# Attention and graph kernel: row sums over one accumulator, softmax weights in five groups

## What is computed

```python
# layer 0: x is (2, 2048, 512), 16 heads of 32
h = ada_ln(x, cond, Wln1, bln1)
x = x + attn(h)           # softmax(q k^T / sqrt(32)) v, then Wo
h = ada_ln(x, cond, Wln2, bln2)
x = x + gelu(h @ W1 + b1) @ W2 + b2
# layer 1, graph attention over the first NG = 20 rows, twice (d = 0, 1)
self_feat = concat(x, q_exp) @ W_self.T + b_self
aff = qh . kh / sqrt(dh) (+ mask and label bias from adj)     # (B, N, H, 20)
w = softmax(aff);  out_t = w @ kv;  out = out_t @ Wout (per head) + bout
x = x + relu(self_feat + out[0] + out[1])
```

## Time and profile before

| | before |
|---|---|
| median of 3 runs | 3079.93 us (3079.63 to 3080.97) |
| the profiled execution | 3083.05 us |
| its span, first to last instruction | 3081.7 us |
| PE busy | 3048.9 us (99%) |
| DVE busy | 2160.9 us (70%) |
| POOL busy | 1545.3 us (50%) |
| ACT busy | 1390.9 us (45%) |
| attention, first to last score | about 334 to 1862 us |
| graph tiles | about 2777 to 3082 us |

### The profile page before, as it was taken

One profiled execution on the slowest core, in us unless ns is written; L12 is line 12 of the kernel. 1 busy time (PEld: TensorE's weight loads), 2 busy tenths in 40 slices (PEclk: granted clock), 3 DMA queues, 4 the chain that ended last, 5 costly groups with the idle time before them and its releaser, 6 DMA issues.

```text
span 3081.7 us, 42809 instructions
## 1 busy us (share of the span) xinstructions
PE 3048.9 (99%) x16058; PEld 2114.3 (69%) x16058; DVE 2160.9 (70%) x3627; ACT 1390.9 (45%) x2705; POOL 1545.3 (50%) x655
## 2 busy tenths in 40 slices
PE   7999999999999999999999999999999999999999
PEld 5887655555555555555555546788888888779998
DVE  5547889898998989989899878643333333247776
ACT  3221566666666666666666673321111111023332
POOL 0000488989889898898988984300000000102222
PEclk9999999999999999999999999999999999899999
DMA  7683787978879788797887868621011111221221
GB/s 230 204 249 123 178 168 166 200 150 189 173 166 200 150 188 173 165 201 150 189 173 160 180 140 253 209 76 36 6 41 42 41 41 30 96 70 63 81 86 57
DMA packets 169365, 423.39 MB, mean 137 GB/s; under 512 B 18492, under 2 KB 60604, under 8 KB 141863
## 3 DMA queue, kind: packets, MB, share of 16 engines
q0 software_dynamic: 27744, 201.08, 32.2%
q1 hardware_dynamic: 139639, 214.07, 23.1%
q10 hardware_dynamic: 1776, 5.51, 0.7%
HBM read 143.51 MB, written 75.50 MB: 71 GB/s over the span
## 4 chain that ended last, share of the span: by engine, by line
PE 94%; DVE 2%; DMA 2%; POOL 1%; issue 0%; ACT 0%; SPq 0%; ACTq 0%; DVEq 0%; POOLq 0%
PE ps L414 16%; PE ps L708 16%; PE ps L719 15%; PE ps L1243 12%; PE ps L1230 11%; PE ps L491 5%; PE ps L1792 4%; PE ps L1809 3%; PE ps L495 3%; PE ps L725 2%; PE ps L1830 1%; DMA x<-in_x 1%; PE ps L1585 1%; PE ps L158 1%; PE ps L1821 1%; PE ps L355 1%
## 5 line engine op out<-in xcount | busy, mean ns | idle before, releaser
L427 DVE TENSOR_REDUCE nmp<-ps 128x1 f32<-128x512 f32 x1966 | 1200.0, 682 | 108.6 <-PE ps L414 104.0
L798 ACT ACTIVATE pt<-ps 128x512 f32<-128x512 f32 x2048 | 1031.0, 625 | 459.1 <-PE ps L708 456.2
L897 POOL TENSOR_TENSOR pt<-pt 128x2048 f32<-128x2048 f32 x217 | 995.5, 4587 | 120.1 <-ACT pt L798 115.0
L708 PE MATMUL ps<-qs,ks 128*128 128x512 f32 x2048 | 810.7, 400 | 2.2 <-ACT pt L798 2.2
L414 PE MATMUL ps<-ks,qs 96*128 96x512 f32 x1966 | 803.9, 409 | 0.1
L414 PEld LDWEIGHTS ps<-ks,qs 96*128 96x128 f32 x1966 | 372.5, 189 | 265.9 <-DVE nmp L427 167.8
L719 PE MATMUL ps<-pt,vq 128*32 128x512 f32 x4096 | 493.8, 600 | 0.0
L708 PEld LDWEIGHTS ps<-qs,ks 128*128 128x128 f32 x2048 | 389.1, 190 | 96.2 <-ACT pt L798 17.7
L1230 PE MATMUL ps<-hpb,w 128*128 128x512 f32 x1536 | 381.3, 398 | 0.0
L1243 PE MATMUL ps<-w,gp 128*128 128x512 f32 x1536 | 379.1, 395 | 1.4 <-DVE gp L1359 1.4
L1357 DVE CAST gp<-g 128x512 fp32r<-128x512 f32 x128 | 61.7, 482 | 393.4 <-ACT g L1346 393.4
(11 more groups left out here) (177 smaller groups left out, 2831.9 us busy)
## 6 DMA issues: line engine op xcount, KB each, us to landing
pt<-pt POOLq DMA_DIRECT2D x189, 1024.0 KB, 8.6
qk_d<-st SPq DMA_DIRECT2D x128, 256.0 KB, 2.9
qs<-qk_d SPq DMA_DIRECT2D x87, 256.0 KB, 4.9
ks<-qk_d SPq DMA_DIRECT2D x42, 512.0 KB, 8.4
xina<-in_x SPq DMA_DIRECT2D x8, 1024.0 KB, 6.6
v_d<-vst SPq DMA_DIRECT2D x32, 256.0 KB, 2.9
vq<-v_d SPq DMA_DIRECT2D x32, 256.0 KB, 4.2
ao_d<-accs SPq DMA_DIRECT2D x32, 256.0 KB, 6.8
```

What stands on the lines that cost most here:

```text
L427: dve.tensor_reduce(nmp[:, n // 4, n % 4:n % 4 + 1], ps[:, ring.bank["max", u], :], AX.X, ALU.max, negate=True).then_inc(s_mr, 1)
L708: pe.matmul(ps[:, score_bank(n), :], ksb[w % 2][:, hh, 128 * kt:128 * kt + 128], qsb[:, v % 3, hh, :], start=True, stop=True).then_inc(s_s ...
L798: act.activation(pt[:, exp_slot(g), hh, :], ps[:, score_bank(n), :], ACT.Exp, scale=SCALE).then_inc(s_exp, 1)
L897: pool.tensor_tensor(accumulator(v, 0), accumulator(v, 0), pt[:, exp_slot(g), :, :], ALU.add).then_inc(s_add, 1)
```

## The change

The row sums of units 0 to 29 are made of one accumulator. In the next unit, ahead of its key tile 3, GpSimd waits for both DMA chains and issues one more DMA that adds accumulator 1 to accumulator 2; at key tile 9 GpSimd adds accumulator 2 to accumulator 0 (`pool_merge`), which it did at tile 15 of the unit itself before. `pe_sums` moves from pair 2 to pair 6 of the next unit, `dve_sums` from pair 3 to pair 7, and multiplies only accumulator 0. Unit 30 keeps its merge at tile 15 and its sums in pair 2 of unit 31, over two accumulators. The merge counts on a semaphore of its own (`s_mg`). The ring of PSUM banks follows the new order.

In the graph, the 640 softmax weights of a row are cut into five groups of 128 columns, whatever the heads (`WG` = 5): five transposes, five matmuls of 128 columns each that overlap their neighbours by 32 columns of output, two copies on ScalarE. `pe_vw` makes a masked 128 x 128 block for each group (40 matmuls of 128 columns for each batch), so `kvr` holds four copies of the keys.

```diff
+WG = 16 * 2 * NG // 128
 def dma_count(v, d, kt):
-    return 16 * (len(ADD_DMA[d]) * v + dma_tiles(v, d).index(kt) + 1)
+    return 16 * (len(ADD_DMA[d]) * v + d * min(v, NU - 2) + dma_tiles(v, d).index(kt) + 1)
+def sums_phase(v):
+    return 6 if v < NU - 2 else 2
 ...
 # pe_sums
-            pe.wait_ge(s_dma[0], dma_count(v, 0, dma_tiles(v, 0)[-1]))
-            pe_ones(bank, accumulator(v, 1), not last, False)
-            pe.wait_ge(s_add, add_count(v, added_tiles(v)[-1]) + (0 if last else 1))
-            pe_ones(bank, accumulator(v, 0), False, True).then_inc(s_end, 1)
+            if v >= NU - 2:
+                pe.wait_ge(s_dma[0], dma_count(v, 0, dma_tiles(v, 0)[-1]))
+                pe_ones(bank, accumulator(v, 1), not last, False)
+            if last:
+                pe.wait_ge(s_add, add_count(v, added_tiles(v)[-1]))
+            else:
+                pe.wait_ge(s_mg, v + 1)
+            pe_ones(bank, accumulator(v, 0), v < NU - 2, True).then_inc(s_end, 1)
 # pe_attention
-                if f == 2 and v:
+                if v and f == sums_phase(v - 1):
                     pe_sums(v - 1)
 # dve_attention
-                if f == 3 and v:
+                if v and f == sums_phase(v - 1) + 1:
                     dve_sums(v - 1)
+        def pool_merge(v):
+            whole = dma_count(v, 1, dma_tiles(v, 1)[-1]) + (16 if v < NU - 2 else 0)
+            pool.wait_ge(s_dma[1], whole)
+            pool.wait_ge(s_add, add_count(v, added_tiles(v)[-1]))
+            pool.tensor_tensor(accumulator(v, 0), accumulator(v, 0), accumulator(v, 2), ALU.add).then_inc(s_mg, 1)
 # pool_attention
+                if 0 < v < NU - 1 and kt == 3:
+                    for d in range(2):
+                        pool.wait_ge(s_dma[d], dma_count(v - 1, d, dma_tiles(v - 1, d)[-1]))
+                    pool.dma_start(accumulator(v - 1, 2), accumulator(v - 1, 1), accum_op=ALU.add).then_inc(s_dma[1], 16)
 ...
-                if v < NU - 1 and kt == 15:
-                    pool.wait_ge(s_dma[1], dma_count(v, 1, dma_tiles(v, 1)[-1]))
-                    pool.wait_ge(s_add, add_count(v, 15))
-                    pool.tensor_tensor(accumulator(v, 0), accumulator(v, 0), accumulator(v, 2), ALU.add).then_inc(s_add, 1)
+                if v == NU - 2 and kt == 15:
+                    pool_merge(v)
+                if 0 < v < NU - 1 and kt == 9:
+                    pool_merge(v - 1)
 # pe_vw
-            for d in range(2):
-                for k in range(NK):
-                    m = pe.matmul(ps[0:120, 1 + b, :], kvr[:, d, b, k, :, :, :], woT[d][:, k, :],
-                                  start=(d == 0 and k == 0), stop=(d == 1 and k == 3))
+            for q in range(WG):
+                if q == 4:
+                    pe.wait_ge(s_rlo, 9 + 3 * b)
+                to = ps[:, 1 + b, 128 * q:128 * q + 128] if q < 4 else ps[:, 5 + b, 0:128]
+                for d in range(2):
+                    for k in range(NK):
+                        keys = kvr[:, d, b, k, :, :, :].rearrange("p h e n -> p (h e n)")
+                        m = pe.matmul(to, keys[:, 8 * q:8 * q + 128], woT[d][:, k, 96 * q:96 * q + 128],
+                                      start=(d == 0 and k == 0), stop=(d == 1 and k == 3))
 # pe_turn_w: range(3 - i) transposes of 128 columns for i in 0, 1
 # pe_heads
-            for q, (h0, nh) in enumerate(HG):
+            for q in range(WG):
                 if q % 3 == 0:
-                    pe.wait_ge(s_wT, 3 * t + 2 * (q // 3) + 1)
-                m = pe.matmul(ps[:, 3 + j, 32 * h0:32 * (h0 + nh)], wT[0:40 * nh, j, q, :],
-                              vw[0:40 * nh, b, q, 0:32 * nh], start=False, stop=(q == 5), skip_group_check=True)
+                    pe.wait_ge(s_wT, 2 * t + q // 3 + 1)
+                m = pe.matmul(ps[:, 3 + j, 96 * q:96 * q + 128], wT[:, j, q, :], vw[:, b, q, :],
+                              start=False, stop=(q == WG - 1), skip_group_check=True)
```

More of the change, by code:

```diff
@@ L1560, in program @@
         wvp = place("wvp", [128, 2, NK, D], held, F32R)
-        vw = place("vw", [120, B, 6, 96], held + 16384)
-        after_vw = held + 16384 + 4 * B * 6 * 96
+        vw = place("vw", [128, B, WG, 128], held + 16384)
+        after_vw = held + 16384 + 4 * B * WG * 128
         gg = place("gg", [128, B, 2, NK, 640], at2 + 24576, F32R)
@@ L1696, in dve_graph_shared @@
                 dve.wait_ge(s_vwm, b + 1)
[L1697 to L1701, removed]
+                for bank, q0, nq in ((1 + b, 0, 4), (5 + b, 4, 1)):
+                    dve.tensor_tensor(vw[:, b, q0:q0 + nq, :].rearrange("p q (h e) -> p (q h) e", e=32),
+                                      ps[:, bank, 0:128 * nq].rearrange("p (h e) -> p h e", e=32),
+                                      bm[:, 4 * q0:4 * (q0 + nq)].unsqueeze(2).to_broadcast([128, 4 * nq, 32]),
+                                      ALU.mult).then_inc(s_vw, 1)
         NX = 5
@@ L1714, in program @@
         ex, junk = whole("ex", 2, 640, at=at1 + 8192), whole("junk", D, at=at1 + 13312)
-        wT = whole("wT", 2, 6, 128, at=at1)
+        wT = whole("wT", 2, WG, 128, at=at1)
         cursor[0] = after_vw
@@ L1817, in pe_turn_w @@
                 if t:
-                    pe.wait_ge(s_wT, 3 * (t - 1) + 2 * i + 1)
-                for q in range(3):
-                    h0, nh = HG[3 * i + q]
-                    m = pe.transpose(ps[0:40 * nh, 5 + i, 128 * q:128 * q + 128],
-                                     ex[:, t % 2, 40 * h0:40 * (h0 + nh)], ident[:, :])
+                    pe.wait_ge(s_wT, 2 * (t - 1) + i + 1)
+                for q in range(3 - i):
+                    c0 = 128 * (3 * i + q)
+                    m = pe.transpose(ps[:, 5 + i, 128 * q:128 * q + 128], ex[:, t % 2, c0:c0 + 128], ident[:, :])
                 m.then_inc(s_tw, 1)
@@ L1872, in act_turn_w @@
         def act_turn_w(t):
-            for r0, q0, q1 in ((120, 0, 3), (120, 3, 4), (80, 4, 6)):
-                act.wait_ge(s_tw, 2 * t + q0 // 3 + 1)
+            for i in range(2):
+                nq = 3 - i
+                act.wait_ge(s_tw, 2 * t + i + 1)
                 if t >= 2:
                     act.wait_ge(s_hd, t - 1)
-                act.activation(wT[0:r0, t % 2, q0:q1, :],
-                               ps[0:r0, 5 + q0 // 3, 128 * (q0 % 3):128 * (q0 % 3 + q1 - q0)].rearrange(
-                                   "p (q n) -> p q n", n=128), ACT.Copy).then_inc(s_wT, 1)
+                act.activation(wT[:, t % 2, 3 * i:3 * i + nq, :],
+                               ps[:, 5 + i, 0:128 * nq].rearrange("p (q n) -> p q n", n=128), ACT.Copy).then_inc(s_wT, 1)
         def act_graph():
@@ L2037, in lay_out @@
     adj = np.stack([mask[:, :, :NG, :], mask[:, :NG, :, :].transpose(0, 2, 1, 3)], axis=2)
-    bm = np.zeros((120, 96), np.float32)
-    for h in range(3):
-        bm[40 * h:40 * h + 40, 32 * h:32 * h + 32] = 1.0
+    bm = np.zeros((128, 4 * WG), np.float32)
+    for q in range(WG):
+        for p in range(128):
+            bm[p, 4 * q + (128 * q + p) // (2 * NG) - 3 * q] = 1.0
     m4 = np.zeros((128, 4), np.float32)
```

13 lines of the change are left out of this document (6 added, 7 removed).

## The result

| | before | after |
|---|---|---|
| median | 3079.78 us (3078.88 to 3080.97, 4 runs) | 3092.72 us (3091.18 to 3097.95, 4 runs) |
| ratio, 95% interval | | 1.0044 [1.0031, 1.0056] |
| span of the profiled execution | 3081.7 us | 3096.6 us |
| attention, first to last score | 1527.4 us | 1548.7 us |
| from there to the first graph score | 915.6 us | 920.3 us |

The change makes the kernel slower by 0.44%, 13 us. The profiled execution of after is the longest of its four, so I take shares of the time from its stages and verdicts from the medians. Attention loses 21.3 us, the stretch from there to the graph tiles (with `pe_vw` in it) 4.7, and the graph tiles win 10.9: +15.1 in the trace.

What follows compares the result with a forecast made beforehand. The prediction took TensorE to bound the kernel, busy 3048.9 of 3081.7 us. Its terms, -7.7 (row sums with pair 3) + 26 (added DMA) - 2 (last units) - 5 (graph) = +11.3, gave 3091 us, range 3063 to 3107.

Steps and rivals of the forecast that it cites:

- rival A: The forecast itself: the key-loading units stall, 3091 us, own range 3078 to 3104; chance 0.50.
- What bounds the kernel: TensorE is busy 3048.9 of 3081.7 us; an edit counts only by shortening its work or making it wait.
- Row sums, TensorE: One accumulator instead of two for v = 0 to 29: 30 x 0.86 = 25.7 us less TensorE work.
- Pair 3: Two reciprocals uncovered in pair 2 make VectorE read maxima 0.62 us later: 29 x 0.62 = 18.0 us given back.
- Rival D: VectorE does not bind either and TensorE keeps the 25.7 us: 3047 us; chance 0.05.
- The added DMA: The extra 1024 KB transfer makes tile 7's DMA late for tile 13's exponential in key-loading units: 13 x 2.0 = +26 us.
- Rivals B and C: B, chance 0.20: the added DMA finds room, 3065 us; C, chance 0.13: half a stall, 1.0 us a unit, 3079.
- Rival E: GpSimd falls behind, its DMAs wait, the merge slips past pair 6 and `pe_sums` waits: 3110 us; chance 0.12.
- Last units: Units 30 and 31: a later merge against earlier reciprocals, product and DMA, sum -2 us (from -4 to +3).
- The +1 for the merge: Unit 30 does v = 29's merge besides its own, so GpSimd ends about 1 us later, where TensorE needs it.
- the -3: Unit 31: VectorE's first add no longer waits for the merge; reciprocals, product and DMA come up to 4 us earlier.
- Graph tiles: Fewer transposes and head matmuls, -0.28 x 32 = -9 us; `pe_vw` +4; sum -5 us (from -6 to +6).

Runs made afterwards that it cites:

- e4: Changed kernel with one reciprocal in each of pairs 0 to 3, GpSimd's product at key tile 7, its store in pair 5: 3133.86 us, ratio 1.0175.
- e6: Kernel of e5 with the four reciprocals in four pairs of e4: 3103.94 us, ratio 1.0071 against before.
- e9: As e4, but GpSimd's product at key tile 6: 3114.77 us, ratio 1.0109 against before.
- e2: Changed kernel, but key loads of units 4 and later fetch 16 columns of 2048, waits and issues kept: 3067.54 us, ratio 0.9956.
- e3: Changed kernel, but the added DMA carries 16 of 512 columns of each head, issue and waits kept: 3062.95 us, ratio 0.9938.
- e7: Kernel of e6 with the four splits of Wo in unit 31 in pairs 2 and 3 instead of 0 and 2: 3102.15 us, ratio 1.0073.
- e5: Changed kernel with six key pieces loaded two to each of three units, in pairs 0 and 1: 3081.83 us, ratio 0.9999.
- e12: As e9, but the store in pair 4, ahead of the third piece of keys: 3090.88 us, ratio 1.0026 against before.
- e10: Before plus graph half, one-accumulator sums only for units 1, 5, ... 29, there four reciprocals and product at key tile 6: 3069.85 us, ratio 0.9970.
- e11: As e10, with one-accumulator sums also for units 2, 6, ... 26: 3066.03 us, ratio 0.9953 against before.
- e1: Kernel before with the graph half of the change alone: 3073.42 us against 3081.60, ratio 0.9976.
- e8: Kernel before with the key pieces placed as in e5, a control: 3081.76 us, ratio 1.0002.

## Why the prediction was right, step by step

Predicted 3091 (3063 to 3107), chance of slower 0.54; measured 3092.7, slower by more than 0.2%. The forecast, rival A, is what happened.

**What bounds the kernel.** Right. GpSimd's and DMA's small margins, not TensorE's 0.86 us, decided.

**Row sums, TensorE.** Right: L731 has 288 matmuls for 528, 0.86 us in pair 6.

**Pair 3.** Right in kind, half too large: 0.62 us forecast, 0.40 measured. The chain in unit 3, from one pair's values to the next:

```profile
484.72 1.85 PE ps L725 x16
490.50 1.85 PE ps L725 x16
496.70 1.85 PE ps L725 x16
```

Pair 3 is 496.70 - 490.50 = 6.20 us, pair 2 5.78. In units 2 to 30 it is 6.17 to 6.22 each time. The prediction took the lag of 0.62 whole. The weight loads in unit 8 (again its timeline) show that a part of it was slack:

```profile
737.44 0.19 PEld L420 LDWEIGHTS ps<-ks,qs 96*128 96x128 f32 x1 [0.21 <-DVE nmp L433]
...
739.22 0.19 PEld L420 LDWEIGHTS ps<-ks,qs 96*128 96x128 f32 x1 [0.30 <-DVE nmp L433]
```

Only the last four of eight loads for maxima are held, by 0.21, 0.29, 0.30 and 0.30 us; these rows are the first and the last of them. So the reading of the earlier trace rows, "there is no slack left in that pair", was wrong by 0.22 us. The term was 18.0 us and measured 29 x 0.40 = 11.6. e4, e6 and e9 show its cause: with one reciprocal per pair, pair 3 is 5.79. Rival D, no such loss, fell. An unstalled unit is so 48.16 - 47.68 = 0.48 shorter, 13.9 over 29 units, where 7.7 was forecast.

**The added DMA.** Right in cause, place and size, and e2 and e3 show it. Forecast 13 x 2.0 = 26 us; measured 13 x (49.88 - 47.68) = 28.6. The parts of it:

- Issue: forecast 9 to 10 us into the unit; in unit 8 at 727.95, 9.4 us.
- Price: unit 8 of after has this row in the DMA view (packets, MB, share of 16 engines), to be read beside the earlier trace rows:

```profile
q0 software_dynamic: 1036, 7.44, 72.9%
```

  72.9% of 51.5 us is 37.5 us for 7.44 million bytes, 5.3 us for a transfer of 1024 KB, where 5.1 was taken.
- The late one is named too narrowly. The prediction followed tile 7's DMA and tile 13. In unit 8 it is tile 5's and tile 11; pair 4, 5 or 6 stalls, from unit to unit. Of ScalarE's 18 waits of 0.4 us or more in units 1 to 29, nine are at tile 9, whose slot is tile 3's: the DMA that stands right behind the added one. The whole queue is late, not one transfer.
- Spread: the 13 units go from 48.15 to 51.57 us, so 2.2 is a mean over very unequal ones.
- What the stall is made of: the score banks absorbed 0.3 us in unit 8 (ScalarE waited 2.00, TensorE 1.72), where 0.5 was taken. TensorE's waits for ScalarE in units 1 to 29 add up to 23.9 - 4.0 = 19.9 us, and three stretches there at the lower clock, 10.2 us in all, cost up to half of that, 5 us. The prediction had no term for the clock, so a part of the agreement of 26 with 28.6 is luck. What makes up the rest was not traced.
- The 16 other units were given 0. They lost 0.23 on average, 3.7 us, all of it in a few of them, such as unit 11 with 1.3.

The sentence on the Trainium skill (DMA: Bandwidth & Descriptors, "Anatomy of one DMA"), by whose fit the term would be near zero, is answered by the 28.6 us: the trace disagrees with it for accumulating DMAs that share the engines with others.

**Rivals B and C** (room, or half a stall) fell: units 8 and 9 are longer than unit 10, and the stall is 2.2 us a unit, where C had 1.0. **Rival E** happened in its first half only: GpSimd's DMAs waited 18 times for the chain, 34.1 us, and in unit 8 the merge began 35.2 us into the unit and ended near 40, but `pe_sums` wants it at 44.6, since it is late by the same stall. In all of attention `pe_sums` waited for a merge once, 0.8 us, and that was unit 31's. The other half of E is not what made e4 slow either: there too `pe_sums` waited for a merge once, 1.9 us, in unit 31.

**Last units.** Wrong: forecast -2, measured +2.8 (unit 30 -0.5, unit 31 +3.3). The +1 for the merge was right, pair 2 of unit 31 being 7.20 us for 6.16. What failed is the -3: "its reciprocals, GpSimd's product and the DMA ... come up to 4 us earlier". In VectorE's program the casts and splits of Wo stand ahead of those. They used to begin 10 us before unit 31; now the copy of the sums, moved to pair 7, stands in front of them and waits for TensorE, and they begin 5 us before the unit, beside an unbroken row of GpSimd adds:

```profile
1835.65 0.69 DVE L832 COPY accs<-ps 128x512 f32<-128x512 f32 x1 [5.53 <-PE ps L731]
1836.25 4.83 DVE L851 CAST wo<-wtmpo 128x512 fp32r<-128x512 f32 x1
1841.12 5.69 DVE L511 TENSOR_TENSOR wo<-wtmpo,wo 128x512 fp32r<-128x512 f32 x1
1846.73 4.81 DVE L851 CAST wo<-wtmpo 128x512 fp32r<-128x512 f32 x1
1851.58 5.06 DVE L511 TENSOR_TENSOR wo<-wtmpo,wo 128x512 fp32r<-128x512 f32 x1
1856.56 1.75 DVE L837 RECIPROCAL accs<-accs 128x128 f32<-128x128 f32 x2
...
1860.38 0.41 DVE L851 CAST wo<-wtmpo 128x512 fp32r<-128x512 f32 x1
1860.82 0.69 DVE L511 TENSOR_TENSOR wo<-wtmpo,wo 128x512 fp32r<-128x512 f32 x1
...
1862.49 1.76 DVE L837 RECIPROCAL accs<-accs 128x128 f32<-128x128 f32 x2
```

Each of the first four ends within 0.6 us of the end of a GpSimd instruction. GpSimd's timeline, then the chain:

```profile
1835.51 5.28 POOL L919 TENSOR_TENSOR pt<-pt 128x2048 f32<-128x2048 f32 x1
...
1840.94 10.32 POOL L919 TENSOR_TENSOR pt<-pt 128x2048 f32<-128x2048 f32 x2
1851.52 4.57 POOL L891 TENSOR_TENSOR pt<-pt 128x2048 f32<-128x2048 f32 x1 [0.26 <-DMA pt<-pt]
...
1864.34 3.21 POOL L884 TENSOR_TENSOR accs<-accv,accs 128x512 f32<-128x512 f32 x1 [7.45 <-DVE accs L837]
```

```profile
1867.50 7.67 DMA pt<-pt
```

The first four took 20.4 us; in before the same four took 7.5, one of them 4.8 beside an add. So VectorE is late, GpSimd's product waits 7.45 us for its reciprocals, and the last DMA of the earlier trace rows is issued 26.5 us into the unit instead of 23.2: the +3.3. The prediction followed the wait for the merge and did not follow the copy that it had itself moved past those casts. e7, which puts the casts behind, agrees in its trace (43.3 to 39.6 us). So do the others, one trace each: where the product begins 23.2 to 24.0 us into unit 31 (after, e2, e3, e5, e6, e12), the unit takes 42.4 to 43.8 us to the end of its last score; where it begins at 21.4 to 22.3 (e4, e7, e9, e10, e11), 39.3 to 40.1. With the attention of before it begins at 19.2 to 20.1 and takes 39.2 us in before, 37.6 in e1 and 36.6 in e8, so the +3.3 rests on one trace of each and could be up to +5.8.

**Graph tiles.** Right, a little better: the chain has `pe_heads` at 1.12 us and a period of 3080.04 - 3071.05 = 8.99, so -0.34 for -0.28 forecast; the stage wins 10.9 for 9. `pe_vw` takes 9.13 and 6.92 us in the chain (the second is cut off at 62 of 80), +4.3 for +4:

```profile
2783.40 9.13 PE ps L1640 x80
...
3069.93 1.12 PE ps L1857 x10
3071.05 3.51 PE ps L1820 x24
...
3078.93 1.12 PE ps L1857 x10
3080.04 3.51 PE ps L1820 x24
```

**Sum.** Forecast against measured: sums with pair 3 -7.7 and -13.9; stalls in key-loading units +26 and +28.6; stalls in others 0 and +3.7; last units -2 and +2.8; graph with `pe_vw` -5 and -6. The measured ones add up to +15, as the trace does; the medians moved by 13. Three terms were off by 4 to 6 us, and one of them had the other sign; part of the closeness of 3091 to 3092.7 is that they cancel.

## What to carry to other kernels

When work is taken off the bounding engine by an extra transfer, count the DMA engines' room in each kind of unit, not as a mean; where one kind is full, make the change only in the others (e11: 14.5 us won, where the change in all units lost 13). Before moving an instruction, list what it was hiding or waiting for: the 1.72 us of sums covered two reciprocals, and a copy moved to pair 7 held up what stood behind it on VectorE. A moved instruction drags others with it, and the order in which two queues get their transfers can be worth more than the edit (e9 against e12, which differ in one store: 1.0109 and 1.0026).

## What the runs showed of the hardware

- **The clock falls behind a stall.** After TensorE waited 1.72 us for ScalarE in unit 8, the granted clock went to the lower level of 1.2 GHz for 3.4 us:

```profile
752.60:757.60 5.00, 4.30 (x20) 1.10 (x21) 1.06 (x3) 2.06 (x4) 4.51 (x2) 0.66 1.05 217
```

  16 value matmuls took 3.50 us for 1.85. Not every stall does this: TensorE waited for ScalarE 22 times in after, 23.9 us in all, with 4 stretches in attention, and 22 times in e4, 48.5 us, with 12. A forecast of stalls of a few us should have a term for it.
- **VectorE's SBUF casts stand still beside a GpSimd add.** 0.41 and 0.69 us alone, 4.8 to 5.7 beside one, ending within 0.6 us of its end; maxima read from PSUM kept their 0.6 us beside the same adds (4.80 for eight at 736.76). The Trainium skill (Advanced Engine Details and Errata, "Mode Summary") says that VectorE's second SBUF port is shared with GpSimd, and that GpSimd's instructions and VectorE's two-port ones block each other. The trace agrees in that the casts stand still; whether the splits, which take 4.9 to 5.7 us beside an add, are two-port ones no run here shows. Reciprocals of SBUF data in pair 2 ran beside adds at 0.88 us each and were not held.
- **Two queues share the DMA engines unevenly.** A piece of keys of 512 KB took 9.6 us or 23.6 us to land, and in the same two units a GpSimd DMA issued 12.0 us into the unit landed at 30.2 or 26.2 us. Over 12 such units the means are 19.0 and 10.4 us for the piece, and 28.4 and 29.6 for the landing (after and e4). By what rule was not settled.
